# Cross-attention of a fused decoder layer: another order of the steps' work, and a second pair of PSUM banks in the output-only steps

## The reference, cut to what matters

```python
scores = qk / math.sqrt(dk)
mean_sim = scores.mean(axis=(-2, -1))
max_sim = scores.max(axis=-1).mean(axis=-1)
probs = softmax(scores, axis=-1)
entropy_proxy = var(probs, axis=-1, ddof=1).mean(axis=-1)
feats = stack([mean_sim, max_sim, entropy_proxy], axis=-1)
hidden = gelu(linear(feats, w1, b1)); hidden = gelu(linear(hidden, w2, b2))
t = exp(clip(linear(hidden, w3, b3), LOG_T_MIN, LOG_T_MAX))[..., None]
attn = softmax(qk / (2.0 * t), axis=-1)
out = linear(merge_heads(attn @ V), Wo, bo)
```

## Time and profile before

| | us |
|---|---|
| median of 3 runs | 1720.15 (1714.52 to 1722.27) |
| the profiled execution, its own time | 1719.28 |
| its span, first to last instruction | 1717.5 |
| TensorE busy with matmuls | 1642.8 (96%) |
| VectorE, ScalarE, GpSimd busy | 1235.7, 926.2, 880.2 |
| mean granted TensorE clock, share of 2.4 GHz | 0.957 |

### The profile page before, as it was taken

One profiled execution on the slowest core, in us unless ns is written; L12 is line 12 of the kernel. 1 busy time (PEld: TensorE's weight loads), 2 busy tenths in 40 slices (PEclk: granted clock), 3 DMA queues, 4 the chain that ended last, 5 costly groups with the idle time before them and its releaser, 6 DMA issues. The chain is left out here.

```text
span 1717.5 us, 42620 instructions
## 1 busy us (share of the span) xinstructions
PE 1642.8 (96%) x14336; PEld 1223.2 (71%) x14336; DVE 1235.7 (72%) x2888; ACT 926.2 (54%) x2189; POOL 880.2 (51%) x1006
## 2 busy tenths in 40 slices
PE   6999999999978999999999999897999999999998
PEld 2555555555546666666666666557999999999998
DVE  5887777777646767766677776436878878787886
ACT  3555545555433666666566666545454545545452
POOL 3444455544446767776677777412433434343342
PEclk9999999999958999998999999788999999999999
DMA  4000000000000000000000000100000000000000
GB/s 123 13 3 2 1 1 1 1 1 1 6 5 4 7 7 7 6 7 6 6 7 7 7 7 5 43 2 1 11 6 9 6 9 6 9 9 6 9 6 13
DMA packets 27869, 16.62 MB, mean 10 GB/s; under 512 B 6193, under 2 KB 25586, under 8 KB 27762
## 3 DMA queue, kind: packets, MB, share of 16 engines
q1 hardware_dynamic: 27762, 15.23, 3.2%
HBM read 9.97 MB, written 4.19 MB: 8 GB/s over the span
## 5 line engine op out<-in xcount | busy, mean ns | idle before, releaser
L1555 POOL TENSOR_TENSOR ff_zz<-ff_zt 128x256 f32<-128x256 f32 x32 | 37.5, 1173 | 318.2 <-DVE ff_zt L1759 318.2
L278 POOL TENSOR_TENSOR sa_KM<-sa_HQK,sc_headmask 128x512 fp32r<-128x512 f32 x64 | 66.7, 1042 | 235.6 <-ACT sa_HQK L318 235.6
L964 ACT ACTIVATE xa_P<-xa_SK 77x1024 f32<-77x1024 f32 x128 | 130.2, 1017 | 98.1 <-PE xa_SK L1287 97.9
L1623 ACT ACTIVATE ff_SG<-bank 128x512 f32<-128x512 f32 x128 | 76.6, 599 | 189.3 <-PE bank L1836 189.3
L1749 DVE TENSOR_TENSOR ff_GL<-ff_GU,ff_GH 128x512 fp32r<-128x512 f32 x128 | 148.6, 1180 | 27.2 <-ACT ff_GH L1628 27.2
L323 ACT ACTIVATE sa_P<-sa_SK 128x1024 f32<-128x1024 f32 x128 | 131.5, 1028 | 59.1 <-PE sa_SK L515 59.1
L409 DVE TENSOR_REDUCE sa_mx<-sa_SQ 128x8 f32<-128x1024 f32 x128 | 156.7, 1224 | 7.6 <-PE sa_SQ L515 5.3
L890 POOL TENSOR_TENSOR xa_QMH<-xa_QBH,xc_headmask 128x512 fp32r<-128x512 f32 x64 | 72.6, 1135 | 151.2 <-ACT xa_QBH L954 151.2
L1901 PE MATMUL bank<-fh_r,ff_GH 128*128 128x256 f32 x512 | 149.2, 292 | 0.0
L1834 PE MATMUL bank<-ff_ZH,fh_b 128*128 128x256 f32 x512 | 146.2, 286 | 0.0
L1903 PE MATMUL bank<-fh_r,ff_GL 128*128 128x256 f32 x512 | 144.5, 282 | 0.0
(11 more groups left out here) (259 smaller groups left out, 5398.3 us busy)
## 6 DMA issues: line engine op xcount, KB each, us to landing
xa_shift<-xa_row SPq DMA_DIRECT2D x256, 2.0 KB
out<-X SPq DMA_DIRECT2D x64, 64.0 KB, 1.5
cx<-ctx SPq DMA_DIRECT2D x64, 38.5 KB
sa_shift<-sa_mT SPq DMA_DIRECT2D x64, 8.0 KB, 1.8
X<-x SPq DMA_DIRECT2D x1, 768.0 KB, 6.7
xa_E<-L_ffn_B SPq DMA_DIRECT2D x2, 256.0 KB, 3.7
xa_E<-down_a SPq DMA_DIRECT2D x1, 512.0 KB, 4.4
X<-x SPq DMA_DIRECT2D x1, 256.0 KB, 2.9
```

Of the source, the lines that this page charges most:

```text
L964: nc.scalar.activation(P[0:TC, (2 * b + h) % 4, :], SK[0:TC, :], ACT.Exp).then_inc(p_ready, 1)
```

## The change

TensorE: the output-side projection of an earlier sample now stands between the picks and the parts of half 0; the inner scores follow the outer ones at once, and the outer ones are two quads in place of three (the third, heads 12 to 16, goes with the inner ones; `ORDER` says which row group each quad of heads uses); output of half 1 moves behind the transposition of x; the transposed maxima come ahead of half 1's picks, and the subtraction between its picks and its parts. In output-only steps half 1 uses two banks of SQ, and the filler is gone except in step 71. Other engines follow with their order. ScalarE keeps `exps` of half 1 ahead of `exp_e`.

```diff
+CROSS_ORDER = (2, 1, 3, 0)
...
+        ALONE = B - LAG
+
+        def by_key_banks(b, h):
+            return SQ[:, 0:1024] if b >= ALONE and h == 1 else SK[:, 0:1024]
...
-                for g in range(QUADS):
+                for place, g in enumerate(ORDER):
                     sp.dma_start(shift[32 * g:32 * g + 1, b % 2].bitcast(F32),
-                                 row[JH * g:JH * g + JH].bitcast(F32)).then_inc(m_row[b % 2], 16)
+                                 row[JH * place:JH * place + JH].bitcast(F32)).then_inc(m_row[b % 2], 16)
...
-                nc.scalar.activation(P[0:TC, (2 * b + h) % 4, :], SK[0:TC, :], ACT.Exp).then_inc(p_ready, 1)
+                nc.scalar.activation(P[0:TC, (2 * b + h) % 4, :], by_key_banks(b, h)[0:TC], ACT.Exp).then_inc(p_ready, 1)
...
             for n in STEPS:
                 r = mlp_round(n)
-                if real(n - LAG):
-                    exps(n - LAG, 0)
                 if real(n - LAG + 1):
                     scaled(n - LAG + 1)
+                if r is not None:
+                    gelu1(r)
+                if real(n - LAG) and r is None:
+                    exps(n - LAG, 0)
                 if real(n + 2):
                     xcT_copy(n + 2)
                 if r is not None:
-                    gelu1(r)
+                    gelu2(r)
                 if real(n - LAG - 1):
                     o_copy(n - LAG - 1)
-                if r is not None:
-                    gelu2(r)
+                if real(n - LAG) and r is not None:
+                    exps(n - LAG, 0)
                 if real(n):
                     mT_copy(n)
                 if real(n + 2):
                     qkv_copy(n + 2)
+                if r is not None:
+                    inverse_t(r)
                 if real(n - LAG):
                     exps(n - LAG, 1)
-                if r is not None:
-                    inverse_t(r)
...
             for n in STEPS:
                 r = mlp_round(n)
-                if real(n - LAG - 2):
-                    residual(n - LAG - 2)
                 if n % 2 == 1 and real(n - 2):
                     inverse_sums((n - 3) // 2)
                 if real(n - 1):
                     sum_e(n - 1)
+                if real(n - LAG - 2):
+                    residual(n - LAG - 2)
                 if real(n - LAG + 1):
                     low(n - LAG + 1)
                 if real(n):
                     row_max(n)
+                if r is not None:
+                    bound(r)
                 if real(n - LAG - 2):
                     stats(n - LAG - 2)
-                if r is not None:
-                    bound(r)
-                if real(n - LAG - 1) and r is None:
+                if real(n - LAG - 1):
                     norm(n - LAG - 1)
+                if real(n + 3):
+                    layernorm(n + 3)
                 if real(n + 2):
                     cast(n + 2)
...
             def scores_outer(b):
...
                 for part in range(3):
-                    scores(b, 0, 4, part, part == 0, part == 2)
-                    scores(b, 8, 12, part, part == 0, part == 2)
-                    last = scores(b, 12, 16, part, part == 0, part == 2)
+                    scores(b, 0, 4, part)
+                    last = scores(b, 8, 12, part)
                 last.then_inc(outer_ps, 1)
 
             def scores_inner(b):
+                scores(b, 12, 16, 0)
                 pe.wait_ge(outer_ps, b + 1)
                 for part in range(3):
-                    scores(b, 4, 6, part, False, part == 2)
-                    last = scores(b, 6, 8, part, False, part == 2)
+                    if part > 0:
+                        scores(b, 12, 16, part)
+                    scores(b, 4, 6, part)
+                    last = scores(b, 6, 8, part)
                 last.then_inc(sq_ps, 1)
...
-            def by_key(b, h, between=None):
-                need(pe, p_ready, 2 * b + h)
+            def by_key(b, h, between):
+                need(pe, p_ready, 2 * b + h if b <= ALONE and h == 0 else 2 * b + h - (b >= ALONE))
+                if b == ALONE and h == 1:
+                    pe.wait_ge(e1_ready, B)
+                banks = by_key_banks(b, h)
...
-                    mm(bank(SK, a), pick[:, r // 32], shift[:, b % 2].rearrange("c j t -> c (j t)"),
+                    mm(bank(banks, a), pick[:, r // 32], shift[:, b % 2].rearrange("c j t -> c (j t)"),
                        start=True, stop=False)
+                between()
...
-                    if part == 0 and between is not None:
-                        between()
...
             for n in STEPS:
                 r = mlp_round(n)
                 if n == 2:
                     pe.wait_ge(pick_set, 1)
-                if n == B:
-                    pe.wait_ge(e1_ready, B)
-                if real(n - LAG - 2):
-                    project(n - LAG - 2)
...
                 if real(n - LAG):
-                    by_key(n - LAG, 0)
+                    by_key(n - LAG, 0, project_last)
+                else:
+                    project_last()
                 if real(n):
                     scores_outer(n)
-                if real(n - LAG - 1):
-                    pv(n - LAG - 1, 1)
+                    scores_inner(n)
                 if r is not None:
                     mlp1(r, n)
                 if real(n + 2):
                     xc_transpose(n + 2)
-                if real(n):
-                    scores_inner(n)
+                if r is not None:
+                    mlp2(r)
+                if real(n - LAG - 1):
+                    pv(n - LAG - 1, 1)
+                elif 2 <= n < LAG:
+                    filler(SK[:, 512:1024], 3)
+                if r is not None:
+                    mlp3(r)
                 if real(n + 2):
                     qkv(n + 2)
-                if r is not None:
-                    mlp2(r)
-                elif real(n - LAG - 1):
-                    if n >= B:
-                        filler(SQ[:, 0:512], 6)
+                if real(n - LAG - 1):
+                    if n >= B + LAG:
+                        filler(SQ[:, 1024:1536], 6)
                     o_transpose(n - LAG - 1, r)
...
+                if real(n):
+                    max_transpose(n)
                 if real(n - LAG):
-                    by_key(n - LAG, 1, maxima)
+                    by_key(n - LAG, 1, subtract)
                 else:
                     if 2 <= n < LAG:
-                        filler(SK[:, 512:1024], 6)
-                    maxima()
-                if r is not None and real(n - LAG - 1):
-                    o_transpose(n - LAG - 1, r)
-                if real(n):
-                    subtract_max(n)
+                        filler(SK[:, 512:1024], 2)
+                    subtract()
...
+    heads_in_order = (JH * np.array(CROSS_ORDER)[:, None] + np.arange(JH)[None]).reshape(-1)
...
-        headsel=(np.arange(128)[:, None] // DK == np.arange(H)[None]).astype(np.float32),
+        headsel=(np.arange(128)[:, None] // DK == heads_in_order[None]).astype(np.float32),
```

More of the change, by code:

```diff
@@ L631, in cross_attention @@
     HIDDEN = slice(3 * T, 3 * T + GROUP * H)
+    ORDER = CROSS_ORDER
     ctx = ExitStack()
@@ L1164, in _ @@
                     row_max(n)
+                if r is not None:
+                    bound(r)
                 if real(n - LAG - 2):
                     stats(n - LAG - 2)
[L1167 to L1169 removed]
+                if real(n - LAG - 1):
                     norm(n - LAG - 1)
+                if real(n + 3):
+                    layernorm(n + 3)
                 if real(n + 2):
                     cast(n + 2)
[L1173 to L1174 removed]
+                if r is not None:
+                    factors(r)
                 if real(n - 1):
                     sum_e2(n - 1)
[L1177 to L1180 removed]
                 if n == -3:
@@ L1226, in _, with scores @@
             PARTS = ((HQ, KMH), (HQ, KML), (LQ, KMH))
-            def scores(b, first_head, last_head, part, start, stop):
-                g = first_head // JH
+            def scores(b, first, last, part):
+                g = ORDER[first // JH]
                 rows = slice(32 * g, 32 * g + 32)
                 queries, keys = PARTS[part]
-                at = first_head // 6 * 512 + first_head % 6 * TC
-                j = first_head % JH
-                n = last_head - first_head
+                at = first // 6 * 512 + first % 6 * TC
+                j = first % JH
+                n = last - first
                 return mm(SQ[:, at:at + n * TC], queries[rows, b % QRING],
-                          keys[rows, b % 2, j:j + n].rearrange("c j k -> c (j k)"), start=start, stop=stop,
-                          skip_group_check=True)
+                          keys[rows, b % 2, j:j + n].rearrange("c j k -> c (j k)"), start=(part == 0 and n == JH),
+                          stop=(part == 2), skip_group_check=True)
             def scores_outer(b):
@@ L1282, in by_key @@
```

(50 more changed lines are left out.)

## The result

The changed kernel takes **1757.98 us** (median of 4 runs, 1751.82 to 1759.73), the kernel before 1720.8 us on the same chip: ratio **1.0217, 95% interval 1.0181 to 1.0253**. It is slower by 37 us, where 11 us less was forecast, and outside the range. The profiled run took 1759.73 us (span 1757.9, mean granted clock 0.926 against 0.957).

A forecast was written before the change was run, and what follows sets the result against it. TensorE was taken to bound ordinary steps (8.49 of 8.58 us busy). Terms -8.6 + 7.7 + 5 - 3 - 12 = -11 us on 1719.3 gave 1709 us; own range 1702 to 1717, full range 1690 to 1737.

The forecast's parts named there:

- +0.35 x 14 = +5: Steps behind rounds: the 1.2 GHz stretch recurs over the denser second half, +5 us; bounds 0 and 18.
- The price itself: Step behind each round: a stretch at 1.2 GHz was said to cost 1.29 us, 9.87 against 8.58.
- The rival of 1692 us: Much faster: denser second half keeps the clock up through three rounds of four, -17 us from the forecast; chance 0.17.
- Output-only steps: -12: Steps 64 to 70: SQ as second bank pair, without filler, shortens 66.4 us to 54; bounds -19 and 0.
- nothing to measure: Output-only steps without filler run at 1.2 GHz throughout, the second bank pair gives nothing: 1721 us; chance 0.13.
- 43 steps x -0.20 = -8.6: Ordinary full steps without a round: period falls from 8.58 to 8.38 us; bounds 8.0 and 8.8.
- +0.55 x 14 = +7.7: Steps with a round: 10.48 grows to 11.03 us, as TensorE waits 1.4 us for SK banks; bounds 10.5 and 11.4.
- Ramp: Steps 0 to 6: inner scores come earlier, 0.3 us per step at full clock, -3 us; bounds 0 and -6.
- Slower, by the clock: New 0.4 us wait before picks lowers the clock in every other ordinary step, +28 us: 1737 us; chance 0.20.
- Slower, by program order: Full steps: outer scores wait for the last by-key part, 57 x 0.45 = +26: 1735 us; chance 0.04.

The follow-up runs named there:

- the experiment: Kernel before with two filler matmuls ahead of the small network's second layer in every step with a round: 1708.82 us, ratio 0.9947.

## Why the prediction was wrong

**The step that failed: the clock, where the forecast put "+0.35 x 14 = +5" with an upper bound of 18.** Against the same schedule at 2.4 GHz (37.05 x 14 = 519) the full steps lost 43 us in the changed kernel. Before, they lost some 7: 528.0 against 14 x (10.44 + 9.61 + 2 x 8.59) = 521 (9.61 as in its steps without a low clock). So the term was about +36. The forecast took a stretch to have one price, 1.3 us, let only its place change, and put +0.35 on that without a row. What happened is that the stretches grew. Before, 11 of the 14 rounds had one. Nine were over after some 3 us, behind which the next step was 0.0 to 0.3 us longer than 9.61; one lasted 7 us (1.6 us in its round) and one 13.7. After, only seven rounds had one, but it filled most of the step behind or all of it, and twice ran on into the next (9.39 and 12.83 us). The row that showed this price was in hand, 14.40 us at 0.53, and was called "once". The seven steps take 13.20 us on average against 8.46, so 4.7 us each and 33 in all; the first and the last full step add 8. All 14 would be 66, far over the bound of 18.

**The price itself was misread.** "Today the step behind each round loses 9.87 - 8.58 = 1.29 us to a stretch at 1.2 GHz": at 2.4 GHz the step still takes 9.61, in the same trace. It was the wait for the onT copy, 0.81 us, of a ScalarE that is late from its table load; at the lower clock TensorE is slow enough to hide that wait, so it showed no idle time. In the run of the experiment the table load of 1.28 us begins at 843.71, just ahead of the subtraction at 843.74, and the exponential (845.00) and the copy (846.07) stand behind it. A low clock and a long step side by side were taken for cause and effect. The rival of 1692 us rested on the same 1.29 and had no ground.

**Output-only steps: -12, with bounds of -19 and 0. Measured +7.6.** The step at 2.4 GHz was nearly right, 6.25 us against 5.96, but only one such step ran at that level. With the filler back the same steps take 6.80 us and the tail 62 to 67. That is 7 to 11 us less than before's 73.5, but most of it is the clock (26 us at 1.2 GHz before, 1 to 9 here): at 2.4 GHz a step gains 7.11 - 6.80 = 0.3 us, and no run separates the pair from the new order in that. The factor for the clock was taken from the old tail, whose filler the change removes; and the worst bound, all at 1.2 GHz, was put at 0, without working it out: a step of 9.9 us against 7.11 would have given a loss. The rival "nothing to measure" had the mechanism right (no filler, so 1.2 GHz throughout) and its price wrong by the same neglect.

**Ordinary step: "43 steps x -0.20 = -8.6". Measured 8.56 or 8.57 against 8.59: about -1.** The chain came as counted, with small misses all one way: transposition of x at S + 1.92 (1.86 forecast), maxima transposed at 3.77 (3.63), second parts at 5.15 (5.09), exponential at 6.16 (6.10), counted from S = 882.46; and from the picks to the next S 1.33 us instead of 1.21. The wait of TensorE ahead of these picks is there, 0.28 us (0.4 forecast), by the exponential as named. That is 0.06 us at the exponential and 0.12 behind it, together the 0.18 between 8.38 and 8.56. The lesson is in the size: a gain of 0.20 stood on a long chain of terms, and misses as small as these were enough to take it away.

**Round: "11.03", so "+0.55 x 14 = +7.7". Measured 11.36** from S to S (862.54 to 873.90; between the subtractions 11.46). The table load began at S + 4.36 rather than 4.16, the second parts at 7.95 rather than 7.74; the wait of 1.31 us was forecast as 1.4. But the late copy behind the round is gone, 9.61 -> 8.46 between subtractions, which the sum did not have, since it had laid those 1.29 us to the clock. The four steps together went from 37.23 to 37.05 us at 2.4 GHz: -0.18 x 14 = -2.5 us of structure, where the forecast had -8.6 + 7.7 = -0.9. Right as a sum, from two terms that were both off.

**Ramp:** -2.3, forecast -3.

**The rivals.** "Slower, by the clock" (0.20, 1737 us) was the right kind, but not at its place: it put a stretch in every other ordinary step, before the 0.28 us wait; ordinary steps away from a round hold 1.00, and with four fillers per round the clock holds although that wait of 0.28 us is still there. The long waits of the rounds lower the clock, and the price of a stretch is up to 5.5 us, not 1.3. The Trainium skill, "TensorE: Matmul & The Clock Gate", section "A second HAM failure mode: psum-queue depth-cycling", says that short idle times between groups of matmuls, if frequent, make the clock oscillate. Here a wait of 0.40 us per round (before, in 11 rounds of 14) and one of 1.31 us (after, in 7 of 14) do that, and filling either stops it for all rounds but one or two; that section gives no price for a stretch. "Slower, by program order" is refuted again: outer scores start at 882.53, 0.07 us behind the first by-key part and ahead of the one at 882.80, which stands before them in the program.

What stays open: why 7 rounds of 14 are followed by a low clock and 7, with the same wait of 1.31 us, are not; and why the stretches last longer than those of before.

## What to carry to other kernels

Cost the clock as a term of its own: for each wait that a change adds or lengthens on a dense TensorE, and for each filler that it removes, work out the stage at 1.2 GHz throughout and put that into the range. A step at the lower level shows TensorE 100% busy and hides the waits that it has at 2.4 GHz, so never read a structural cost as the difference of two steps at different clocks. And before a schedule is reordered, try a few short useless matmuls in its waits: here 0.7 to 1.1 us of them per round gave 0.5% in the old kernel and, with those of the tail, 3% in the new one (1758 to 1705). They won back what the clock had cost; the reordering itself has not been shown to gain anything.

## What was not expected of the hardware

In the tail without filler the low level lasted 82 us in one piece although TensorE was busy for 9.51 of 10 us: at 1.2 GHz it looks fully used, and still it is not granted the higher clock. With six filler matmuls per step the tail ran at 0.93 to 0.99, by the run. Runs of one kernel also spread with their mean clock: 1719 to 1749 us with the tail's filler back, 1700 to 1709 with both fillers (four matmuls per round).
